# The token-step operations and running sums of a second sequence, placed on other engines and in another step of a one-core Mamba-2 and gated-MLP kernel

## The chip, the cores and the metric

The kernel runs on one core of one Trainium2 chip. A time is the device time of one execution in microseconds (us); the lower the better. TensorE (PE) multiplies matrices, VectorE (DVE), ScalarE (ACT) and GpSimd (POOL) do the element-wise work, and SyncE (SP) issues most transfers. Each engine works through its own instruction stream in order; the streams meet at semaphores alone.

## What is computed

For two sequences of 512 tokens of width 512, `x` is normalised, and then `x + s * silu(ffn)` is formed. `ffn` is a gated MLP with four-bit weights. `s` is a Mamba-2 layer with 128 heads of 64 channels in 8 groups. Cut to what matters here:

```python
proj = hidden_states @ in_proj_w.T
gate, xBC, dt = jnp.split(proj, [INTER, INTER + CONV_DIM], axis=-1)
xBC = silu(causal_conv(xBC, conv_w, 4) + conv_b)
x, Bm, Cm = jnp.split(xBC, ...)
dt = jnp.clip(jax.nn.softplus(dt + dt_bias), 0.001, 100.0)
dA = dt * A                      # A = -(1 .. 128), one per head
cs = jnp.cumsum(dA, axis=-1)     # within chunks of 128 tokens
scores = (C @ B.T) * where(tril, exp(cs_l - cs_s), 0)
Y = scores @ (x * dt) + C @ states * exp(cs) + x * D
out = rmsnorm_per_group(Y * silu(gate)) * norm_w @ out_proj_w.T
```

The change concerns `dt`, `dA` and `cs` of the second sequence.

## The kernel before

A **body** is one of 16 pairs of sequence and head group (the two sequences alternate), and a body has eight **steps** `k` of 128 channels (two heads) each; `n = 8 * body + k` numbers the steps. Each engine has a function `step(body, k)`, and `over_bodies` (line 96) calls it for n = 0, 1, 2, ... on every engine. All matrices that meet weights are split into a high and a low part, so that one product is three matmuls (`split_mm`, line 140).

In a step TensorE does, in order: `y_off` (L590, L573 in the trace, the state's share of the output of the step before), `conv` (the projection for three steps ahead, L143 to L145), `y_diag` (`diag`, L609, and `state_mm`, L573), `gate_mm` (the gate two steps ahead), `out_mm` (L677 to L679), `extra` (at k = 3 and 4 the B and C projections of the next body, at 6 and 7 more small ones) and `turn_x` (L738). At n = 2 and 3 the order differs a little (lines 765 to 774): at n = 2 there is no `out_mm`, and at n = 3 `second_values` (L808, transposes L805) stands ahead of `y_diag`, and two `out_mm` follow `gate_mm`.

VectorE does in a step: `xdt`, `xw` and `ec` (L1306, L1309, L1315), then at n = 1 `token_steps(dve, 1)`, at n = 2 `smallest` once (L1267), at n = 3 `stage_hp(1)` (L1443) and `smallest` twice; then `inner` (L1360, writes `yt`), the state recurrence (L1379, L1384), `taps_x_conv` (L1246, three multiply-adds), at n = 1 `cumulate(1)`, and last, in the crowded steps n = 1, 2 and 3, `scores` (L1280).

`token_steps(eng, b)` (line 352) is three operations on 128x512 numbers of sequence `b`: the sum that completes the softplus (L356), the clip (L359) and the product with A (L362). It waits for `pa` (ScalarE's logarithm, `soft_ln(1)`, L1076, at n = 0) and `pd` (VectorE's `relu_dt(1)`, ahead of the steps). `cumulate(b)` (line 1430) is four scans of 128x128 (L1433), one for each chunk; they raise `pd`.

Who waits for the scans:

- ScalarE, in `first_steps` at k = 2: after `raw_x_conv` (L1000) and `round_x` (L901) comes `send_sums(1)` (line 1078), which waits for all scans and issues the transfer of `cs` to `cs_d`; then `decays(1)` (L1083, four L1085, and the transfer to `e_d`), then `work_a` (L964, eight exponentials for the scores), `round_out`, `rest`. At k = 3 come `stage_hp(1)` (L1096), `raw_x_conv`, `round_x`, `work_a` and so on; `gate_raw` (L987) moves a gate out of PSUM and raises `gev_done`.
- GpSimd, at n = 1, between the low part of the convolution's weights (L1611) and that of the gate's (L1627): `pool.wait_ge(pd, SEQS * N_PD)`, with no work behind it. At n = 2 `weigh(1)` (L1549: L1551, L1553) waits for `pa` (that is, for `decays(1)`) and `pd`.
- TensorE, at n = 3: `second_values` waits for `wg_done`, that is for `weigh(1)`.

GpSimd does in a step: `gated` (L1594, L1598), L1611, the low parts of the B and C, gate and output weights (L1620, L1627, L1631), the sum of squares (L1604) and `low_y` (L1578, which raises `lo_done`). VectorE's `inner(k)` writes `yt[k % 2]` and so waits for the `low_y` that read it (`lo_done`, line 1358), besides TensorE's `diag` (`yd_done`).

Of the kernel before, what the change touches and what calls it, by code (L numbers as in the profile page):

```python
# [26 lines left out]
SEQS, SEQ, DIM = 2, 512, 512  # L27
# [52 lines left out]
def at(body, k, d):  # L80

    k += d
    return body.plus(k // TILES), k % TILES


def wait(eng, sem, count):

    if isinstance(count, int) and count <= 0:
        return
    eng.wait_ge(sem, count)  # L90
# [18 lines left out]
def paired(n):  # L109

    return TILES // 2 <= n < TILES * (BODIES - 1) + TILES // 2
# [47 lines left out]
def build(nc, x, w_conv, w_gate, w_out, w_dt, conv_p, norm_p, head_p, consts, w1q, w1s, w3q, w3s,  # L159
# [9 lines left out]
    with ExitStack() as ctx:  # L169
        def sem(name):  # L170
            return ctx.enter_context(nc.semaphore(name))
# [112 lines left out]
        pd = sem("pd")  # L284
# [67 lines left out]
        def token_steps(eng, b):  # L352

            eng.wait_ge(pa, (N_SOFT + N_EXPS) * b + N_SOFT)
            eng.wait_ge(pd, N_PD * b + 1)
            eng.tensor_tensor(qt[Q_DT][:, half[b], :], qt[Q_DT][:, half[b], :], ecs[:, half[b], :],  # L356
                              ALU.add).then_inc(dt_done, 1)
            eng.wait_ge(dt_done, 3 * b + 1)
            eng.tensor_scalar(qt[Q_DT][:, half[b], :], qt[Q_DT][:, half[b], :], DT_MIN, DT_MAX, ALU.max,  # L359
                              ALU.min).then_inc(dt_done, 1)  # L360
            eng.wait_ge(dt_done, 3 * b + 2)
            eng.tensor_scalar(qt[Q_CD][:, half[b], :], qt[Q_DT][:, half[b], :], heads[:, 2:3], None,  # L362
                              ALU.mult).then_inc(dt_done, 1)
# [4 lines left out]
        N_PD = 1 + NC  # L368
# [21 lines left out]
        def sq_tile(kp):  # L390

            return sq_sum[:, :] if kp == 0 else gate[:, kp % 4, :]
# [845 lines left out]
        def _(dve):  # L1238
# [21 lines left out]
            def smallest(body, k):  # L1260
                bd, kr = at(body, k, 2)
                if bd.exists():
                    m = TILES * bd.n + kr
                    if kr == 0:
                        wait_hp(dve, bd)
                    dve.wait_ge(row_in[m % LM_BUFS], 16 * (m // LM_BUFS + 1))
                    dve.scalar_tensor_tensor(lm[m % LM_BUFS][:, :, :],  # L1267
                                             hp[bd.seq][:, Q_CS, kr, :].unsqueeze(2).broadcast_to((P, 2 * NC, CHUNK)),
                                             -1.0, lm[m % LM_BUFS][:, :, :], ALU.mult, ALU.min).then_inc(min_done, 1)
# [13 lines left out]
            def step(body, k):  # L1283
                n = TILES * body.n + k
# [53 lines left out]
                                                 ALU.mult, ALU.add).then_inc(acc_done, 1)  # L1338

                if n == 1:  # L1340
                    token_steps(dve, 1)
                elif n == 2:
                    smallest(body, 1)
                elif n == 3:
                    stage_hp(1)
                    smallest(body, 2)
                    smallest(body, 3)
                else:
                    smallest(body, k)
# [13 lines left out]
                def taps_x_conv():  # L1363
                    bd, kx = at(body, k, 3)
                    if bd.exists():
                        taps(bd, X_POS[kx], z[:, kx % 2, :], ps_a, tap0_x, taps_x, TILES * bd.n + kx)
# [23 lines left out]

                if not (paired(n) and k % 2):
                    taps_x_conv()
                if n == 1:
                    cumulate(1)
                if crowded:
                    scores(body, k)
# [33 lines left out]
            def cumulate(b):  # L1430
                dve.wait_ge(dt_done, 3 * (b + 1))
                for c in range(NC * b, NC * b + NC):
                    dve.tensor_tensor_scan(qt[Q_CS][:, c, :], ones[:, :], qt[Q_CD][:, c, :], 0.0, ALU.mult,  # L1433
                                           ALU.add).then_inc(pd, 1)

            def stage_hp(b):
                if b:
                    dve.wait_ge(hp_out, 16 * b)
                for q in (Q_DT, Q_DEC):
                    dve.wait_ge(qt_tr, NQ * b + q + 1)  # L1440
                    if b == 0:
                        dve.wait_ge(hp0_ev, q + 1)
                    dve.tensor_copy(stage[:, q, :, :, :].rearrange("p g k (j c) -> p c (g k) j", c=NC),  # L1443
                                    qt_bank[q][:, :].rearrange("p (c u j) -> p c u j", c=NC, j=2)).then_inc(qt_ev, 1)
# [90 lines left out]
        def _(pool):  # L1535
# [45 lines left out]
            def step(body, k):  # L1581
                n = TILES * body.n + k
                pv, kp = at(body, k, -1)
                before = body.plus(-1)
                if k == 1 and before.exists():
                    pool.wait_ge(rs_done, before.n + 1)
                    wait(pool, acc_done, NC * before.n)
                    pool.tensor_tensor(rstd[:, :], rstd_sum[:, :], neg_half[:, 0:NC], ALU.pow).then_inc(rv_done, 1)
                chain_late = paired(n) and k % 2

                def gated():
                    pool.wait_ge(t0_done, n)
                    pool.wait_ge(y1_done, n)
                    pool.tensor_tensor(yt[:, kp % 2, P:SEQ], yt[:, kp % 2, P:SEQ], ec[kp % 2][:, :], ALU.add  # L1594
                                       ).then_inc(add_done, 1)
                    pool.wait_ge(gs_done, n)
                    pool.wait_ge(add_done, n)
                    pool.tensor_tensor(yt[:, kp % 2, :], yt[:, kp % 2, :], gate[:, kp % 4, :], ALU.mult  # L1598
                                       ).then_inc(yg_done, 1)

                def sum_sq():
                    pool.wait_ge(sq_done, n)
                    wait(pool, sqa_done, (TILES - 1) * pv.n + kp - 1)
                    pool.tensor_tensor(sq_sum[:, :], sq_sum[:, :], sq_tile(kp), ALU.add).then_inc(sqa_done, 1)  # L1604

                if pv.exists() and not chain_late:
                    gated()
                bd, kx = at(body, k, 4)
                if bd.exists():
                    pool.wait_ge(whi_x, TILES * bd.n + kx + 1)  # L1610
                    pool.tensor_tensor(conv_lo[kx % 2][:, :, :],  # L1611
                                       raw_x[:, kx % 2, :].rearrange("p (k j) -> p k j", k=KT),
                                       conv_hi[kx % 2][:, :, :].bitcast(F32), ALU.subtract).then_inc(wlo_x, 1)
                if paired(n) and k == 0:
                    sum_sq()
                if n == 2:
                    weigh(1)
                for bd, i in bc_piece(body, k):
                    pool.wait_ge(whi_b, 2 * bd.n + i + 1)
                    pool.tensor_tensor(conv_lo[2][:, :, :], bc_raw(bd).rearrange("p (k j) -> p k j", k=KT),  # L1620
                                       conv_hi[2][:, :, :].bitcast(F32), ALU.subtract).then_inc(wlo_b, 1)
                if n == 1:

                    pool.wait_ge(pd, SEQS * N_PD)
                for group, pos in gate_piece(body, k):
                    pool.wait_ge(whi_g, 8 * group + pos + 1)
                    pool.tensor_tensor(gate_lo[pos // 4][:, pos % 4, :], raw_g[:, :],  # L1627
                                       gate_hi[pos // 4][:, pos % 4, :].bitcast(F32), ALU.subtract).then_inc(wlo_g, 1)
                for group, pos in out_piece(body, k):
                    pool.wait_ge(whi_o, TILES * group + pos + 1)  # L1630
                    pool.tensor_tensor(wout_lo[pos // 4][:, pos % 4, :], raw_o[:, :],  # L1631
                                       wout_hi[pos // 4][:, pos % 4, :].bitcast(F32), ALU.subtract).then_inc(wlo_o, 1)
                if chain_late:
                    gated()
                low_first = (body.is_number(BODIES - 1) and k >= 5) or body.is_number(BODIES) or chain_late
                if low_first and pv.exists():
                    low_y(body, k)
                if pv.exists() and kp > 0 and body.exists() and not (paired(n) and k == 0):
                    sum_sq()
                if pv.exists() and not low_first:  # L1640
                    low_y(body, k)
                if k == 6 and body.is_number(0):
                    pool.wait_ge(hp_out, 16 * SEQS)
                    pool.wait_ge(qt_tr, NQ * SEQS)
                    pool.memset(acc[:, :, :], 0.0).then_inc(zero_done, 1)
# [156 lines left out]
```

## Time and profile before

| | us |
|---|---|
| median of 3 runs | 1759.21 (1757.86 to 1759.34) |
| the profiled execution's own time | 1758.21 |
| its span in the trace | 1756.4 |
| TensorE busy | 1742.4 (99%) |
| VectorE busy | 1402.7 (80%) |
| ScalarE busy | 1221.6 (70%) |
| GpSimd busy | 1232.1 (70%) |

All rows come from the one profiled execution, whose time is 1.8 us above its span. The start times in a timeline count from the span's start. Instructions of one engine overlap by some 0.06 to 0.1 us in the records, so distances between starts say more than sums of durations.

### The profile page before, as it was taken

The page shows a single profiled execution, that of the slowest core. Times are in us where ns is not written, and L with a number is a line of the kernel's source. Part 1 is how long each engine was busy: PE and PEld are TensorE (multiplying, and loading weights), DVE is VectorE, ACT ScalarE, POOL GpSimd, SP SyncE. Part 2 cuts the span into 40 slices and gives each one's busy share as a digit, 9 for nine tenths or more (in the row PEclk, how much of TensorE's full clock was granted, in tenths as well). Part 3 has the DMA queues.
Part 4 walks back from the last instruction along what each step waited for, and adds up shares of the span by engine and source line. Part 5 has one row for each costly group of instructions (what it writes and reads, how often), then busy time and mean ns, then how long its engine had stood idle before and what let it go on. Part 6 is the DMA issues. An engine that isn't in the chain of part 4 may idle for free.

```text
span 1756.4 us, 30305 instructions
## 1 busy us (share of the span) xinstructions
PE 1742.4 (99%) x10301; PEld 1459.3 (83%) x10301; DVE 1402.7 (80%) x2211; ACT 1221.6 (70%) x2456; POOL 1232.1 (70%) x877
## 2 busy tenths in 40 slices
PE   8999999999999999999999999999999999999999
PEld 6788888888888888888888888888888888888877
DVE  7978788878878788778788788878887887868941
ACT  6986677777776777777867778767877787643320
POOL 5677777777876787677776777677777787576630
PEclk9999999999999999999999999999999999999999
DMA  5442333333333343333333333333323343236522
GB/s 196 165 131 99 116 116 112 98 123 109 134 105 94 104 135 109 108 101 117 118 102 118 116 111 108 103 109 127 123 91 103 109 135 107 76 98 175 146 78 96
DMA packets 122595, 202.84 MB, mean 115 GB/s; under 512 B 23056, under 2 KB 60560, under 8 KB 122192
## 3 DMA queue, kind: packets, MB, share of 16 engines
q1 hardware_dynamic: 120720, 197.32, 34.8%
q10 hardware_dynamic: 1728, 3.65, 0.5%
q8 instruction: 82, 1.34, 0.3%
q14 instruction: 65, 0.53, 0.1%
HBM read 193.57 MB, written 7.34 MB: 114 GB/s over the span
## 4 chain that ended last, share of the span: by engine, by line
PE 94%; DVE 3%; issue 1%; POOL 1%; DMA 0%; ACT 0%; SPq 0%; DVEq 0%; ACTq 0%; POOLq 0%
PE bank L143 17%; PE bank L145 16%; PE bank L144 16%; PE bank L573 10%; PE bank L609 7%; PE bank L677 7%; PE bank L679 7%; PE bank L678 6%; PE bank L888 3%; PE bank L738 3%; DVE z L1246 1%; PE bank L700 0%; DVE lm L1267 0%; PE bank L720 0%; DVE acc L1337 0%
## 5 line engine op out<-in xcount | busy, mean ns | idle before, releaser
L964 ACT ACTIVATE lm<-lm,hp 128x128 f32<-128x128 f32 x1024 | 313.1, 389 | 0.8
L1246 DVE SCALAR_TENSOR_TENSOR z<-bank,cw_all,z 128x511 f32<-128x511 f32 (+2 forms) x384 | 286.9, 747 | 13.3 <-ACT z L1000 4.2
L1611 POOL TENSOR_TENSOR conv_lo<-raw_x,conv_hi 128x512 fp32r<-128x512 f32 x124 | 203.7, 1643 | 129.4 <-ACT conv_hi L901 129.3
L143 PE MATMUL bank<-xn_hi,conv_hi 128*128 128x512 f32 x640 | 261.4, 408 | 1.9 <-DVE z L1246 1.4
L1306 DVE TENSOR_TENSOR xdt<-bank,hp 128x512 f32<-128x512 f32 x128 | 88.2, 689 | 212.4 <-PE bank L738 212.4
L145 PE MATMUL bank<-xn_hi,conv_lo 128*128 128x512 f32 x640 | 250.6, 392 | 0.0
L144 PE MATMUL bank<-xn_lo,conv_hi 128*128 128x512 f32 x640 | 249.5, 390 | 0.0
L1594 POOL TENSOR_TENSOR yt<-yt,ec 128x384 f32<-128x384 f32 x128 | 146.8, 1147 | 139.3 <-DVE ec L1315 107.9
L1280 DVE SCALAR_TENSOR_TENSOR lm<-lm,gm 128x1024 f32<-128x1024 f32 x128 | 225.3, 1760 | 7.8 <-ACT lm L964 7.2
L1578 POOL TENSOR_TENSOR y_lo<-yt,y_hi 128x512 fp32r<-128x512 f32 x128 | 180.1, 1407 | 52.4 <-ACT y_hi L1035 52.4
L143 PE MATMUL bank<-xn_hi,gate_hi 128*128 128x512 f32 x512 | 212.9, 416 | 0.0
L677 PE MATMUL bank<-wout_hi,y_hi 128*128 128x512 f32 x512 | 206.1, 403 | 0.0
L1598 POOL TENSOR_TENSOR yt<-yt,gate 128x512 f32<-128x512 f32 x128 | 192.1, 1500 | 18.9 <-POOL yt L1594 0.9
L1604 POOL TENSOR_TENSOR sq_sum<-sq_sum,gate 128x512 f32<-128x512 f32 x111 | 172.7, 1556 | 40.3 <-ACT gate L1041 40.2
L679 PE MATMUL bank<-wout_hi,y_lo 128*128 128x512 f32 x512 | 200.8, 392 | 0.0
L144 PE MATMUL bank<-xn_lo,gate_hi 128*128 128x512 f32 x512 | 200.3, 391 | 0.0
L145 PE MATMUL bank<-xn_hi,gate_lo 128*128 128x512 f32 x512 | 200.2, 391 | 0.0
L678 PE MATMUL bank<-wout_lo,y_hi 128*128 128x512 f32 x512 | 199.5, 390 | 0.0
L987 ACT ACTIVATE gate<-bank 128x512 f32<-128x512 f32 x128 | 75.0, 586 | 173.4 <-PE bank L145 173.4
L1267 DVE SCALAR_TENSOR_TENSOR lm<-hp,lm 128x1024 f32<-128x1024 f32 x128 | 185.9, 1453 | 0.0
L1000 ACT ACTIVATE z<-bank,cw_all 128x512 f32<-128x512 f32 x128 | 98.6, 770 | 101.8 <-PE bank L145 100.9
L145 PEld LDWEIGHTS bank<-xn_hi,conv_lo 128*128 128x128 f32 x640 | 120.1, 188 | 26.6
(152 smaller groups left out, 4051.5 us busy)
## 6 DMA issues: line engine op xcount, KB each, us to landing
lm<-cs_d SPq DMA_DIRECT2D x128, 512.0 KB, 4.5
raw_x<-w_conv_dram SPq DMA_DIRECT2D x128, 256.0 KB, 3.5
ec<-e_d SPq DMA_DIRECT2D x256, 96.0 KB, 2.7
raw_o<-w_out_dram SPq DMA_DIRECT2D x64, 256.0 KB, 3.0
raw_g<-w_gate_dram SPq DMA_DIRECT2D x61, 256.0 KB, 3.2
raw_g<-w_conv_dram SPq DMA_DIRECT2D x16, 256.0 KB, 3.2
raw_o<-w_conv_dram SPq DMA_DIRECT2D x14, 256.0 KB, 3.4
q_raw<-w1q_dram SPq DMA_DIRECT2D x10, 256.0 KB, 3.9
```

Of the source, the lines that this page charges most:

```text
L143: pe.matmul(dst, a_hi, b_hi, start=(i == 0), stop=False)
L144: pe.matmul(dst, a_hi, b_lo, start=False, stop=False)
L145: mm = pe.matmul(dst, a_lo, b_hi, start=False, stop=(i == len(terms) - 1))
L677: pe.matmul(ps_o[c][:, :], y_hi[:, ko % 2, o], w[0], start=first, stop=False)
L678: pe.matmul(ps_o[c][:, :], y_hi[:, ko % 2, o], w[1], start=False, stop=False)
L679: mm = pe.matmul(ps_o[c][:, :], y_lo[:, ko % 2, o], w[0], start=False, stop=last)
L964: e = act.activation(lm[m % LM_BUFS][:, u, :], lm[m % LM_BUFS][:, u, :], ACT.Exp, bias=hp[bd.seq][:, Q_CS, k1, u:u + 1])
L1246: dve.scalar_tensor_tensor(dst[:, d:SEQ], src[:, 0:SEQ - d], cw_all[:, bd.group, pos, 3 - d:4 - d], dst[:, d:SEQ], ALU.mult, ALU.add).then ...
L1267: dve.scalar_tensor_tensor(lm[m % LM_BUFS][:, :, :], hp[bd.seq][:, Q_CS, kr, :].unsqueeze(2).broadcast_to((P, 2 * NC, CHUNK)), -1.0, lm[m ...
L1280: dve.scalar_tensor_tensor(lm_c, lm_c, 1.0, gm[:, :, :].rearrange("p c l -> p (c l)").unsqueeze(1) .broadcast_to((P, 2, SEQ)), ALU.mult, A ...
L1598: pool.tensor_tensor(yt[:, kp % 2, :], yt[:, kp % 2, :], gate[:, kp % 4, :], ALU.mult).then_inc(yg_done, 1)
L1611: pool.tensor_tensor(conv_lo[kx % 2][:, :, :], raw_x[:, kx % 2, :].rearrange("p (k j) -> p k j", k=KT), conv_hi[kx % 2][:, :, :].bitcast(F ...
```

## The change

At n = 1 the three operations of `token_steps` of the second sequence leave VectorE's stream and stand in GpSimd's, where its wait for the scans stood; that wait is gone. VectorE's four scans of that sequence stand in n = 2 and not in n = 1: behind the taps, ahead of `scores`. ScalarE's, TensorE's and SyncE's streams are the same.

```diff
@@ VectorE, step
                 if n == 1:
-                    token_steps(dve, 1)
+                    pass
                 elif n == 2:
                     smallest(body, 1)
@@ VectorE, step, behind the state recurrence
                 if not (paired(n) and k % 2):
                     taps_x_conv()
-                if n == 1:
+                if n == 2:
                     cumulate(1)
                 if crowded:
                     scores(body, k)
@@ GpSimd, step
                 if n == 1:
-
-                    pool.wait_ge(pd, SEQS * N_PD)
+                    token_steps(pool, 1)
                 for group, pos in gate_piece(body, k):
```

## Rows read from the trace of the kernel before

**Rows 1.** The page: TensorE's busy time, its share and its instructions.
```profile
PE 1742.4 (99%) x10301; PEld 1459.3 (83%) x10301; DVE 1402.7 (80%) x2211; ACT 1221.6 (70%) x2456; POOL 1232.1 (70%) x877
```
**Rows 2.** Waits of TensorE, 40 to 300 us: total, times, longest.
```profile
PE bank L143 <- DVE z L1246: 1.4, 2, 0.9
PE bank L609 <- DVE ec L1315: 0.8, 1, 0.8
PE bank L738 <- DVE state L1384: 0.5, 1, 0.5
```
**Rows 3.** Windows: stretch, busy PE, PEld, DVE, ACT, POOL; granted clock, DMA, GB/s.
```profile
82.00:94.00 12.00, 12.00 (x59) 9.82 (x59) 7.96 (x13) 11.69 (x28) 10.64 (x7) 1.00 0.55 194
```
**Rows 4.** Timeline of VectorE, sequence 0's scans, then n = 1 to 2: start, us, line.
```profile
21.99 1.37 DVE L1433 TENSOR_TENSOR_SCAN qt<-ones,qt 128x128 f32<-128x128 f32 x4
...
56.77 0.68 DVE L356 TENSOR_TENSOR qt<-qt,ecs 128x512 f32<-128x512 f32 x1
...
59.96 0.73 DVE L1360 SCALAR_TENSOR_TENSOR yt<-xt,dc_all,bank 128x512 f32<-128x512 f32 x1
60.62 0.28 DVE L1379 COPY state<-bank 128x128 f32<-128x128 f32 x1
...
64.06 1.36 DVE L1433 TENSOR_TENSOR_SCAN qt<-ones,qt 128x128 f32<-128x128 f32 x4
65.34 1.20 DVE L1280 SCALAR_TENSOR_TENSOR lm<-lm,gm 128x1024 f32<-128x1024 f32 x1
...
67.98 2.01 DVE L1267 SCALAR_TENSOR_TENSOR lm<-hp,lm 128x1024 f32<-128x1024 f32 x1
71.25 0.75 DVE L1360 SCALAR_TENSOR_TENSOR yt<-xt,dc_all,bank 128x512 f32<-128x512 f32 x1 [1.25 <-issue]
...
75.36 1.73 DVE L1280 SCALAR_TENSOR_TENSOR lm<-lm,gm 128x1024 f32<-128x1024 f32 x1
```
**Rows 5.** Timeline of TensorE: products of n = 1, diagonal of n = 2, projection of n = 3.
```profile
58.38 1.09 PE L609 MATMUL bank<-lm,xdt 128*64 128x128 f32 x16
59.40 0.94 PE L573 MATMUL bank<-xw,b_tok 128*128 128x128 f32 x6
...
68.12 1.09 PE L609 MATMUL bank<-lm,xdt 128*64 128x128 f32 x16 [0.83 <-DVE ec L1315]
...
90.26 0.50 PE L143 MATMUL bank<-xn_hi,conv_hi 128*128 128x512 f32 x1
```
**Rows 6.** Timeline of GpSimd: one cast ahead of the steps, then n = 1.
```profile
40.21 0.61 POOL L1568 CAST gate_hi<-raw_g 128x512 fp32r<-128x512 f32 x1 [1.07 <-DMA raw_g<-w_gate_dram]
...
59.86 1.32 POOL L1611 TENSOR_TENSOR conv_lo<-raw_x,conv_hi 128x512 fp32r<-128x512 f32 x1
65.50 2.18 POOL L1627 TENSOR_TENSOR gate_lo<-raw_g,gate_hi 128x512 fp32r<-128x512 f32 x1 [4.32 <-DVE qt L1433]
...
68.88 2.27 POOL L1578 TENSOR_TENSOR y_lo<-yt,y_hi 128x512 fp32r<-128x512 f32 x1
```
**Rows 7.** Timeline of ScalarE: sequence 0's wait for its scans; then n = 1 to 3.
```profile
23.78 2.06 ACT L1057 ACTIVATE xn_hi<-bank 128x512 fp32r<-128x512 f32 x4 [1.24 <-DVE qt L1433]
...
63.45 0.61 ACT L928 ACTIVATE gate_hi<-raw_g 128x512 fp32r<-128x512 f32 x1
...
68.53 0.62 ACT L1083 ACTIVATE ecs<-qt 128x512 f32<-128x512 f32 x1
...
70.22 2.44 ACT L964 ACTIVATE lm<-lm,hp 128x128 f32<-128x128 f32 x8
...
79.99 2.09 ACT L1096 ACTIVATE stage<-bank 128x512 f32<-128x512 f32 x2 [1.03 <-PE bank L805]
...
89.63 0.58 ACT L987 ACTIVATE gate<-bank 128x512 f32<-128x512 f32 x1
```
**Rows 8.** Timeline of TensorE ahead of the steps: transposes at the kernel's start, and later.
```profile
4.05 4.60 PE L816 MATMUL bank<-ident 128*128 128x128 f32 x24 [4.05 <-DMA ident<-consts_dram]
...
21.05 1.91 PE L787 MATMUL bank<-ident,x_in 128*128 128x128 f32 x16
```

## The prediction

> **What bounds the kernel now.** I read the page first: TensorE is busy for 99% of the span [rows 1], so time is won or lost only where TensorE stands still, or comes to stand still. The list of TensorE's waits between 40 and 300 us comes next [rows 2]: four stalls, 2.7 us in all, and all of them before 76 us, in steps n = 1 to 3, where the change lies. Each is put down to VectorE. From 82 us on TensorE is busy without a break and at a granted clock of 1.00, its upper level of 2.4 GHz, but ScalarE is busy there too, for 11.69 of 12 us [rows 3]. The reader is to see that two engines are full at once behind the change: TensorE, and ScalarE, which feeds it.
>
> So I looked for the point where they meet. In step 3 TensorE starts the B projection of the next body at 90.26 us [rows 5]; it needs PSUM that ScalarE's `gate_raw` empties, and that instruction ends at 89.63 + 0.58 = 90.21 [rows 7]. ScalarE comes just in time: whatever makes it later than this makes TensorE later by the same amount. How much can ScalarE lose before that point? Between 68.53 and there its only idle time is 1.03 us at 79.99 [rows 7], where it waits for TensorE's transposes of the second sequence; I count 1.1 with the overlap of records.
>
> **The change, part by part.**
>
> *Step 1, VectorE.* The three operations begin at 56.77 and `inner` behind them at 59.96, so 3.2 us go [rows 4]. Little of it is kept at once: `inner` waits for the diagonal products, which end at 58.38 + 1.09 = 59.5, and the state copy waits for the state products, 59.40 + 0.94 = 60.35 [rows 5], where it stood at 60.62 [rows 4]. The scans go too. The scores then start at 60.38 + (64.06 - 60.62) = 63.8 and not at 65.34: 1.5 us earlier. The stall of 0.8 us ahead of the diagonal [rows 2] should go: `ec`, now 0.05 ahead of the diagonal at 68.12 [rows 5], moves with the scores to 66.5, before the projection ends at 67.2.
>
> *Step 1, GpSimd.* After L1611 ends at 61.2 it now works where it waited 4.32 us [rows 6]. The trace has no large `tensor_scalar` on GpSimd. The first operation, with two inputs, is like L1611, 1.3. For the two with one input I take the cast of the same size, 0.61 each, with 1.3 as the upper end; 0.61 is nearest, since it too reads one tensor and writes one. That gives 61.2 + 1.3 + 1.2 = 63.7, and the next piece, L1627, can't start before ScalarE's rounding ends at 64.06 [rows 7] anyway. At the upper end it starts at 65.1, still before the 65.50 of now.
>
> The trace shows something dearer. L1627 lasts 2.18 where it meets VectorE's scores (65.34 to 66.54), L1578 lasts 2.27 where it meets `smallest` of 2.01 [rows 4, 6]: such pairs run one after the other. So I put them in turn: scores to 65.0, L1627 to 66.3, the output weights (1.3) to 67.5, `smallest` to 68.7, L1578 to 69.9. The two bounds: no such meeting, 67.9; operations of 1.3 us, with scores between them, 71.0. The Trainium skill states this in "GPSIMD Engine Reference", Key points: the SBUF interfaces are shared with VectorE, in contention with its instructions with two SBUF inputs. By that rule the trace agrees, 2.18 and 2.27 against 1.32. The same page's Engine selection speaks against moving such work: GpSimd takes about twice as long for two inputs and is near line rate for one; by it, as an estimate, the three would take what I took at the lower end.
>
> *Step 2, VectorE.* Its `inner` starts now at 71.25, just behind L1578's end at 71.15 [rows 4, 6]. In the new kernel that end is 69.9, not below 68.4 (the diagonal, at 68.12 behind 0.83 of idleness now, starts at 67.3 and takes 1.09 [rows 5]), not above 71.1 by the sum above. From `inner` to the end of the taps is 75.36 - 71.25 = 4.1 [rows 4]: 74.0. There the scans stand now, 1.36 [rows 4]: they end at **75.4 (73.9 to 76.6)**.
>
> *Step 2, ScalarE.* This is the cost. Its stream did not change: behind L901 it waits for the scans before it sends the sums. They ended at 65.4 and it went by at 68.53 without a stop [rows 4, 7]. Now it stands from 68.6 until 75.4. Everything behind the wait stands with it: the decays, eight exponentials, output weights, silus, `y_hi`, `gate_raw`. From the end of the scans to its next work are 0.42 us for sequence 0 (scans to 23.36, issue of the transfer, next activation at 23.78 [rows 4, 7]); from the decays to the exponentials 70.22 - 68.53 = 1.69. So the exponentials start at 75.4 + 0.4 + 1.7 = 77.5, for 70.22 now: **ScalarE is 7.3 us late (5.8 to 8.5)**.
>
> *Step 3.* Who waits: GpSimd's `weigh`, for the decays; TensorE's 16 transposes for `weigh`; VectorE's scores for the exponentials (until 80.0), and behind them xdt, xw and ec; so the diagonal of n = 3 starts near 83 instead of 80.3, and the next gate projection near 85.8 instead of 82.0 for `gate_raw` of n = 2. None of it is the last. ScalarE's idle 1.1 at 79.99 is gone, since the transposes are done by 82: it is 6.2 late (4.7 to 7.4) from there on, and `gate_raw` of n = 3 ends at 96.4. TensorE's two `out_mm` end near 94, so it waits for ScalarE, and starts the B projection 6.2 us late. The two transfers, `cs_d` and `e_d`, are issued 7 us later; their first readers are the rows of body 1, steps away. SyncE's queue waits for GpSimd's and VectorE's counts and shifts with them by no more.
>
> *Behind.* TensorE had no idle time from 82 us on to win the delay back [rows 2, 3], and the 2.7 us of stalls that VectorE no longer causes lie ahead of the new, longer waits and are swallowed by them. The sum: +6.2 us, 1758.21 + 6.2 = 1764.4 against the profiled execution. That one lies 1.0 below the median of the runs; I add half of that: **1764.9 us**.
>
> **The rivals.**
>
> *VectorE is what counts, and the change helps.* All of TensorE's stalls here are put down to VectorE [rows 2], and 4.5 us leave its step 1. If ScalarE's stop costs nothing, the three later stalls vanish (0.8, 0.5 and the longer one of 0.9): -2.3 us, 1756.4 by my base, the same within measurement. It decides at the scans' end: by 69.7 (68.6 plus the 1.1 of slack) ScalarE loses nothing. Against it: `inner` alone can't start before 68.4, and 5.5 us of VectorE's work stand behind it. Chance 0.12, most of it for a reading of mine of who waits that is wrong.
>
> *GpSimd's one-input operations are slow.* At 3 us each they end at 68.5; L1627, the output weights and L1578 follow with one meeting, 73.2; `inner` then, scans to 78.7, ScalarE 9.5 us late after its slack: 1768.2. For: only tiny ones are in the trace. Against: the cast, 0.61 [rows 6]. Chance 0.12.
>
> *TensorE's clock falls in the new gaps.* It would stand for 2 us several times between 77 and 96. The first 24 transposes, after TensorE had stood still from the start, took 4.60 us; at 1.91/16 each they take 2.87 [rows 8]. A start from rest costs 1.7, and only the last gap's counts, the earlier ones being behind ScalarE: +7.9, 1766.6. Against: between the gaps it works for 8 us. "TensorE: Matmul & The Clock Gate" (the Trainium skill, What's actually happening) has the slow clock come back after idleness; no row here shows it inside the work. Chance 0.05.
>
> *The change doesn't do what it says*, because ScalarE meets the scans earlier than I order them: that is the first rival, as the stream order is plain in the diff.
>
> **How the numbers follow.** My forecast has 0.71. With its bounds it alone spans 1758.7 + 4.7 to 1758.7 + 7.4 = 1763.4 to 1766.1; half a microsecond to a whole one of spread between runs and the slow-GpSimd case widen it upward to 1768.0, downward a part hidden by something I have not seen, to 1762.0. A measurement tells about 0.2% here, 3.5 us: all but the first rival and a thin edge of the forecast are slower by more. Faster by over 0.2% has 0.02, within 0.2% 0.13, slower 0.85.
>
> **What would show it.** In the profile of the changed kernel: scans near 74 to 75.4; ScalarE idle for 6 to 7 us ahead of L1083, released by L1433, as it was 1.24 for sequence 0 [rows 7]; three GpSimd lines at 61.2 to 64; next to no idle ahead of L1627; TensorE waiting before the transposes L805, the diagonal, a gate projection and the B projection, together some 9 us in place of 2.3; from then on every row as before, 6.2 us later. The forecast is wrong if ScalarE's wait is there and TensorE's B projection starts near 90 all the same, or if the scans end before 70.

## The result, and the profile after

The changed kernel takes 1767.2 us (median of 6 runs, 1765.57 to 1767.99) against 1758.85 for the kernel before (6 runs, 1757.86 to 1760.19): a ratio of 1.0046, 95% interval 1.0033 to 1.0059. It is slower by 8 us, and the direction, the place and the mechanism are those of the forecast of 1764.9 (1762.0 to 1768.0), with the size short by 2.3 us.

The page of the changed kernel, span and busy times. TensorE has the same work (1743.7 us busy for 1742.4) in a span 9.7 us longer:

```profile
span 1766.1 us, 30304 instructions
PE 1743.7 (99%) x10301; PEld 1460.2 (83%) x10301; DVE 1400.7 (79%) x2208; ACT 1221.7 (69%) x2456; POOL 1235.1 (70%) x880
```

TensorE's waits in the changed kernel (total, times, longest), of the whole span; they answer to [rows 2]. The wait for ScalarE's `gate` and most of those for `state` and `qt` are new:

```profile
PE bank L143 <- ACT gate L987: 3.2, 2, 2.0
PE bank L738 <- DVE state L1384: 2.8, 2, 1.7
PE bank L805 <- POOL qt L1553: 2.7, 2, 2.3
PE bank L143 <- DVE z L1246: 1.4, 2, 0.9
PE bank L609 <- DVE ec L1315: 1.3, 1, 1.3
```

The timeline of ScalarE (start, us, line, operation, idle time before and what ended it), for [rows 7]. It stands for 8.8 us ahead of the decays, until the scans are done; the idle 1.03 ahead of L1096 is gone; `gate_raw` of n = 3 begins 8.3 us later than before:

```profile
78.03 0.63 ACT L1083 ACTIVATE ecs<-qt 128x512 f32<-128x512 f32 x1 [8.82 <-DVE qt L1433]
79.74 2.43 ACT L964 ACTIVATE lm<-lm,hp 128x128 f32<-128x128 f32 x8
88.37 2.02 ACT L1096 ACTIVATE stage<-bank 128x512 f32<-128x512 f32 x2
97.94 0.57 ACT L987 ACTIVATE gate<-bank 128x512 f32<-128x512 f32 x1
```

The timeline of TensorE, the first projection matmul of n = 1 and the B projection of n = 3, for [rows 5]:

```profile
56.28 0.47 PE L143 MATMUL bank<-xn_hi,conv_hi 128*128 128x512 f32 x1 [0.46 <-DVE z L1246]
...
98.57 0.50 PE L143 MATMUL bank<-xn_hi,conv_hi 128*128 128x512 f32 x1 [2.04 <-ACT gate L987]
```

All of the first body is 0.8 us late in this execution, ahead of the change (56.28 for 55.48 us). The cause stands at the start of VectorE's timeline: the statistics of one of the first tiles of `x` wait for its transfer. First the kernel before, then the changed one:

```profile
6.16 0.69 DVE L1404 BATCH_NORM_STATS2 bn<-x_in 128x6 f32<-128x512 f32 x1 [0.16 <-DMA x_in<-x_dram]
```

```profile
6.92 0.69 DVE L1404 BATCH_NORM_STATS2 bn<-x_in 128x6 f32<-128x512 f32 x1 [0.84 <-DMA x_in<-x_dram]
```

In seven of the experiments this row stands between 6.11 and 7.31 us, and in all nine executions the first matmul of n = 1 follows 49.3 to 49.5 us behind it. The 24 opening transposes [rows 8] vary too (5.29 us here for 4.60), but they don't set it: they last 4.49 us in e9_scans_early_held and 5.38 in e3_scans_early, and both start n = 1 at 56.0. There is one profile for each kernel, so whether this lateness has to do with the kernel is not shown; it lies ahead of the change.

So I read distances inside the body. From the first to the second of these two rows I call **D**. D was 90.26 - 55.48 = 34.8 us; it is now 42.3: **7.5 us more, in a stretch in which the matmuls are the same.**

The timeline of VectorE, for [rows 4]: `smallest`, `inner`, the scans and the scores of n = 2. Inner starts at 72.16, that is 71.4 in the clock of before; the scans last 1.36 us and end at 77.6; the scores stand for 4.57 us behind ScalarE's exponentials:

```profile
67.32 2.34 DVE L1267 SCALAR_TENSOR_TENSOR lm<-hp,lm 128x1024 f32<-128x1024 f32 x1
72.16 0.75 DVE L1360 SCALAR_TENSOR_TENSOR yt<-xt,dc_all,bank 128x512 f32<-128x512 f32 x1 [2.50 <-issue]
...
76.26 1.36 DVE L1433 TENSOR_TENSOR_SCAN qt<-ones,qt 128x128 f32<-128x128 f32 x4
82.20 1.23 DVE L1280 SCALAR_TENSOR_TENSOR lm<-lm,gm 128x1024 f32<-128x1024 f32 x1 [4.57 <-ACT lm L964]
```

The timeline of GpSimd, for [rows 6]. The two `tensor_scalar` last 1.93 and 1.98 us, where VectorE took 1.13 and 1.39 for them in n = 1; they end at 67.3, `low_y` (L1578) at 72.06, and `inner` starts 0.1 behind it:

```profile
63.33 1.93 POOL L359 TENSOR_SCALAR qt<-qt 128x512 f32<-128x512 f32 x1
65.35 1.98 POOL L362 TENSOR_SCALAR qt<-qt,heads 128x512 f32<-128x512 f32 x1
67.30 1.28 POOL L1626 TENSOR_TENSOR gate_lo<-raw_g,gate_hi 128x512 fp32r<-128x512 f32 x1
68.54 2.27 POOL L1630 TENSOR_TENSOR wout_lo<-raw_o,wout_hi 128x512 fp32r<-128x512 f32 x1
70.78 1.28 POOL L1578 TENSOR_TENSOR y_lo<-yt,y_hi 128x512 fp32r<-128x512 f32 x1
```

### The profile page after: what moved, and what is told of

Its sections match the earlier page's. It is cut to its first block, busy times and chain, and to the rows that moved or that the text cites. A ratio compares the mean times of both kernels' runs of the same rounds, so it can differ in the third digit from the quotient of the medians.

```text
span 1766.1 us, 30304 instructions
## 1 busy us (share of the span) xinstructions
PE 1743.7 (99%) x10301; PEld 1460.2 (83%) x10301; DVE 1400.7 (79%) x2208; ACT 1221.7 (69%) x2456; POOL 1235.1 (70%) x880
## 4 chain that ended last, share of the span: by engine, by line
PE 89%; DVE 3%; POOL 2%; ACT 2%; issue 2%; DMA 1%; SPq 0%; ACTq 0%; POOLq 0%; DVEq 0%
PE bank L143 16%; PE bank L145 16%; PE bank L144 16%; PE bank L573 10%; PE bank L609 6%; PE bank L677 6%; PE bank L679 6%; PE bank L678 6%; PE bank L888 3%; PE bank L738 3%; ACT lm L964 1%; DVE z L1246 1%; POOL conv_lo L1611 0%; DMA raw_g<-w_gate_dram 0%; PE bank L700 0%
## 5 line engine op out<-in xcount | busy, mean ns | idle before, releaser
L1594 POOL TENSOR_TENSOR yt<-yt,ec 128x384 f32<-128x384 f32 x128 | 145.5, 1136 | 138.9 <-DVE ec L1315 107.5
L1578 POOL TENSOR_TENSOR y_lo<-yt,y_hi 128x512 fp32r<-128x512 f32 x128 | 180.1, 1407 | 52.6 <-ACT y_hi L1035 52.6
L1598 POOL TENSOR_TENSOR yt<-yt,gate 128x512 f32<-128x512 f32 x128 | 191.6, 1497 | 18.4
L143 PEld LDWEIGHTS bank<-xn_hi,conv_hi 128*128 128x128 f32 x640 | 120.6, 188 | 26.2 <-ACT gate L987 2.5
```

The source lines that it names most:

```text
L143: pe.matmul(dst, a_hi, b_hi, start=(i == 0), stop=False)
```

## The experiments

The theories. **A**: the cost is ScalarE's stop for the late scans. **B**: it is GpSimd's slower operations and what they hold back. **C**: TensorE waits for the second sequence's weights, whatever ScalarE does. After the first four runs came theory **D** (D without the word "theory" is always the distance): GpSimd and a VectorE operation with two inputs in SBUF take turns, so that where the scans stand decides what they last.

### The three operations alone on GpSimd (e1_tokens_only)

```diff
-                if n == 2:
+                if n == 1:
                     cumulate(1)
```

> The changed kernel with the scans back in n = 1: the three operations on GpSimd alone. Measure D = from the first matmul of the projection of n = 1 (L143) to that of the B projection of n = 3: 34.8 us before, 42.3 in the changed kernel. Theory A (the cost is ScalarE's stop for the late scans): the scans end some 1.5 us before ScalarE asks for them, no stop, D 34 to 35.5, time within 1.5 us of before. Rival B (the cost is GpSimd's slower operations and what they delay: output weights, low_y): most of the 7.5 us stay, D 40 or more.

Measured: 1763.97 us (8 runs) against 1759.24 of before in the same series (26 runs), ratio 1.0028 (1.0017 to 1.0039), +4.7 us; the distance D = 96.78 - 56.15 = 40.6, 5.8 more than before. A's numbers are missed and B's is met, though not by B's mechanism. The timelines of GpSimd, VectorE, ScalarE and TensorE:

```profile
63.16 1.93 POOL L359 TENSOR_SCALAR qt<-qt 128x512 f32<-128x512 f32 x1
65.18 1.58 POOL L362 TENSOR_SCALAR qt<-qt,heads 128x512 f32<-128x512 f32 x1
...
66.80 4.49 DVE L1433 TENSOR_TENSOR_SCAN qt<-ones,qt 128x128 f32<-128x128 f32 x4 [2.22 <-POOL qt L362]
...
71.69 0.63 ACT L1083 ACTIVATE ecs<-qt 128x512 f32<-128x512 f32 x1 [2.65 <-DVE qt L1433]
...
73.99 1.98 PE L609 MATMUL bank<-lm,xdt 128*64 128x128 f32 x16 [6.28 <-DVE ec L1315]
```

The operations end at 66.7, so VectorE sits idle for 2.2 us; and then the four scans last 4.49 us, not 1.36. Behind them are the scores, the multiplications of n = 2 and `ec`, and TensorE stands for 6.3 us. ScalarE's stop is only 2.65 us, with 1.61 more behind it for `smallest`, and TensorE doesn't wait for ScalarE ahead of the B projection. So this kernel pays in another coin: not what GpSimd does next (its `low_y` begins at 69.3, earlier than in the changed kernel), but VectorE, waiting for GpSimd and then scanning beside it.

### The scans alone in n = 2 (e2_scans_only)

```diff
                 if n == 1:
-                    pass
+                    token_steps(dve, 1)
@@ GpSimd
-                if n == 1:
-                    token_steps(pool, 1)
```

> The changed kernel with the three operations back on VectorE in n = 1 and nothing in their place on GpSimd: the late scans alone. Theory A: VectorE's inner of n = 2 starts about 1.5 us earlier than in the changed kernel, ScalarE still stops for some 6 to 7.5 us, D 40 to 41, +5.5 to +6.5 us over before. Rival B: D 34 to 36, +0 to +1.

Measured: 1764.68 us (7 runs), ratio 1.0035 (1.0024 to 1.0047), +5.4 us; D = 97.06 - 56.13 = 40.9, 6.1 more than before. A holds (its time of +5.5 to +6.5 is missed by 0.1). The timelines of VectorE (`inner` of n = 2) and ScalarE:

```profile
70.65 0.75 DVE L1360 SCALAR_TENSOR_TENSOR yt<-xt,dc_all,bank 128x512 f32<-128x512 f32 x1 [1.25 <-issue]
76.53 0.63 ACT L1083 ACTIVATE ecs<-qt 128x512 f32<-128x512 f32 x1 [7.25 <-DVE qt L1433]
```

`Inner` starts at 70.65 (70.0 in the clock of before, 14.5 behind the first matmul; 15.9 in the changed kernel), ScalarE's stop is 7.25 us. The late scans alone make 6.1 of the 7.5 us. The rest, 1.4, is what `inner` loses by GpSimd's two slow operations.

### The scans ahead of `smallest` in n = 2 (e3_scans_early)

```diff
                 elif n == 2:
+                    cumulate(1)
                     smallest(body, 1)
@@
-                if n == 2:
-                    cumulate(1)
                 if crowded:
```

> The changed kernel with the four scans at another place in n = 2: ahead of smallest, not behind the taps. GpSimd's three operations as in the changed kernel. Theory A: the scans end near 68.7 in that trace's clock, ScalarE's stop shrinks from 8.8 us to under 1, D 34.5 to 35.5, time within 1.5 us of before. Rival B: D 40 or more, since GpSimd does what it does in the changed kernel.

Measured: 1763.31 us (10 runs), ratio 1.0023 (1.0013 to 1.0033), +4.1 us; D = 94.53 - 56.03 = 38.5. Half of the loss came back, not all. The timelines of VectorE (the scans) and TensorE (behind the gate projection of n = 2):

```profile
67.11 5.31 DVE L1432 TENSOR_TENSOR_SCAN qt<-ones,qt 128x128 f32<-128x128 f32 x4
...
76.64 1.09 PE L738 MATMUL bank<-ident,xt 128*128 128x128 f32 x4 [4.37 <-DVE state L1385]
```

The scans begin at 67.1, as meant, and last 5.31 us, 1.17 to 1.50 each. They end at 72.4: ScalarE still stops for 3.9 us, and VectorE is late with all behind them, for which TensorE waits 4.4 us. Neither A nor B had room for that; it started theory D.

### ScalarE does other work first (e5_decays_behind_exps)

```diff
-                if k == 2:
-                    send_sums(1)
-                    decays(1)
                 ...
                 round_out(body, k)
+                if k == 2:
+                    send_sums(1)
+                    decays(1)
                 rest(body, k)
```

> The changed kernel with ScalarE's sending of the sums and its decays of the second sequence placed behind the exponentials and output weights of n = 2, not ahead of them. The scans end as late as in the changed kernel. Theory A: 3.7 us of ScalarE's work move into its stop, which shrinks from 8.8 to about 5.1; D falls by 3.7 to 38.6, the time to +4 to +5 over before. Rival C (TensorE waits for the weights of the second sequence, that is for the decays through GpSimd and the 16 transposes, whatever ScalarE does between): D stays at 42.

Measured: 1762.79 us (10 runs), ratio 1.0021 (1.0012 to 1.0031), +3.6 us; D = 95.08 - 56.36 = 38.7. D is what A says (38.6), the time a little under its +4 to +5, and C falls: the scans end as late as ever (77.7 for 77.6), the weights pass through the decays, GpSimd and TensorE as late as ever (the transposes L805 start at 81.90 for 81.78), and half of the loss is gone. ScalarE's timeline ahead of the decays:

```profile
73.60 0.72 ACT L943 ACTIVATE raw_o<-raw_o,nw_all 128x512 f32<-128x512 f32 x1 [1.36 <-DMA raw_o<-w_out_dram]
...
78.13 0.63 ACT L1083 ACTIVATE ecs<-qt 128x512 f32<-128x512 f32 x1 [3.15 <-DVE qt L1433]
```

The stop is 3.15, less than the 5.1 expected, but 1.36 us of it moved ahead, where ScalarE now waits for a load, and 0.5 ahead of the exponentials.

### GpSimd held while VectorE scans (e9_scans_early_held)

e3_scans_early and one line:

```diff
                 if n == 1:
                     token_steps(pool, 1)
+                    pool.wait_ge(pd, SEQS * N_PD)
```

> As e3_scans_early, with GpSimd's wait for the scans put back behind its three operations in n = 1, so that GpSimd does nothing while VectorE scans. Theory D (the two engines take turns: a scan with two inputs in SBUF lets one GpSimd operation through each, 1.3 us a scan): the four scans take 1.4 us and not 5.3; GpSimd's next pieces start later (68.5 in place of 67.0), yet D (from the first matmul of the projection of n = 1 to that of the B projection of n = 3) falls from 38.5 to about 36.4, time +1 to +2.5 over before. Rival E (the scans were slow for what they read, freshly written by GpSimd): they still take 4 us or more and D is 39 to 40.

Measured: 1761.02 us (11 runs) against 1758.94 (23 runs), ratio 1.0014 (1.0005 to 1.0023), +2.1 us; D = 92.26 - 55.99 = 36.3. A wait was added, and D fell from 38.5 to 36.3 and the time from +4.1 to +2.1. The intervals of the two ratios overlap, so that it gains rests on D more than on the times. The timelines of VectorE and TensorE:

```profile
67.06 1.37 DVE L1432 TENSOR_TENSOR_SCAN qt<-ones,qt 128x128 f32<-128x128 f32 x4
...
70.73 0.50 PE L143 MATMUL bank<-xn_hi,gate_hi 128*128 128x512 f32 x1 [1.27 <-POOL gate_lo L1626]
75.38 0.63 PE L738 MATMUL bank<-ident,xt 128*128 128x128 f32 x4 [1.64 <-DVE state L1385]
```

The same scans on the same data, written by GpSimd as before, last 1.37 us: rival E falls, theory D holds. The price of the hold is in the two other rows: TensorE waits 1.3 us for GpSimd's low part of the gate weights and 1.6 for the state.

### The kernel before without GpSimd's wait (e4_no_wait)

```diff
-                if n == 1:
-
-                    pool.wait_ge(pd, SEQS * N_PD)
```

> The kernel before with one line taken away: GpSimd's wait for the scans in n = 1. It doesn't idle the 4.3 us. Theory D: the scans, 1.36 us now, meet three GpSimd operations and take 3.5 to 5 us; VectorE is 2 to 3.5 us late in n = 2 and the diagonal of n = 2 with it; D 36 to 38, time +1 to +3. Rival F (the wait was only a cost): scans 1.4 us, low_y earlier, D 33.5 to 34.5, time -1.

Measured: 1761.72 us (11 runs), ratio 1.0018 (1.0009 to 1.0027), +2.8 us; D = 94.46 - 56.02 = 38.4, against 36 to 38 expected. The timelines of VectorE, GpSimd and TensorE:

```profile
64.59 4.50 DVE L1433 TENSOR_TENSOR_SCAN qt<-ones,qt 128x128 f32<-128x128 f32 x4
...
64.69 1.41 POOL L1624 TENSOR_TENSOR gate_lo<-raw_g,gate_hi 128x512 fp32r<-128x512 f32 x1 [2.97 <-ACT gate_hi L928]
66.06 1.42 POOL L1628 TENSOR_TENSOR wout_lo<-raw_o,wout_hi 128x512 fp32r<-128x512 f32 x1
67.43 1.38 POOL L1578 TENSOR_TENSOR y_lo<-yt,y_hi 128x512 fp32r<-128x512 f32 x1
...
71.80 1.98 PE L609 MATMUL bank<-lm,xdt 128*64 128x128 f32 x16 [3.96 <-DVE ec L1315]
```

Three GpSimd operations run beside the scans and are hardly slower (1.41, 1.42, 1.38 for 1.29), while the scans take 4.50 for 1.36: the first, ahead of them, 0.41, the other three 1.42 to 1.46, one scan for each operation. The diagonal runs at the lower clock (1.98 us for 1.09), which no theory had. The wait of 4.32 us in [rows 6], which looks like pure loss, was worth 2.8 us; without it GpSimd still stands for 2.97, until ScalarE's rounding.

### The scans in VectorE's idle time (e7_scans_behind_smallest)

```diff
                 elif n == 2:
                     smallest(body, 1)
+                    cumulate(1)
@@
-                if n == 2:
-                    cumulate(1)
                 if crowded:
```

> The changed kernel with the scans behind smallest in n = 2, where VectorE sat idle for 2.5 us waiting for low_y. Theory D: GpSimd works there too (output weights, low_y, the gated output), so the scans take 4 to 5 us instead of 1.4; they end near 74.5, ScalarE's stop is some 6 us and inner is 2 to 3 us late; D 39 to 41. Rival: they fill the idle time at 1.4 us, end near 71.2, D 37 or less.

Measured: 1764.34 us (6 runs), ratio 1.0030 (1.0018 to 1.0042), +5.4 us; D = 96.29 - 56.69 = 39.6. VectorE's timeline:

```profile
69.98 5.35 DVE L1432 TENSOR_TENSOR_SCAN qt<-ones,qt 128x128 f32<-128x128 f32 x4
```

As theory D says (D 39 to 41; the scans last 0.35 more than its 4 to 5): they fill the 2.5 us of idleness and 2.8 more, and ScalarE stops for 6.1. The idleness was not free: GpSimd worked in it.

### The first sequence's operations on GpSimd (e6_tokens0_pool)

```diff
-            token_steps(dve, 0)
@@ GpSimd, ahead of its wait for sequence 0's scans
+            token_steps(pool, 0)
```

> The kernel before with the three operations of the FIRST sequence on GpSimd, which stands idle there for 5.0 us, while VectorE has nothing with two SBUF inputs to do behind norm. For their durations alone: if GpSimd's tensor_scalar is slow by itself, they last 1.9 and 1.6 us here as well, against 0.43 and 0.49 on VectorE; if the 1.9 of the changed kernel came from meeting VectorE, some 0.6 to 1.3. The first B and C pieces come 3 to 4 us later, part of it hidden by TensorE's weightless matmuls.

One run, 1762.67 us, against 1758.94 of before. GpSimd's timeline, with VectorE idle through the second and the third:

```profile
22.70 1.93 POOL L359 TENSOR_SCALAR qt<-qt 128x512 f32<-128x512 f32 x1
24.73 1.58 POOL L362 TENSOR_SCALAR qt<-qt,heads 128x512 f32<-128x512 f32 x1
```

1.93 and 1.58 us with nothing on VectorE beside them, the same as in e1_tokens_only, where the first met VectorE's taps. VectorE has 0.43 and 0.49 for the two at the same place. `tensor_scalar` on GpSimd is slow by itself; of the changed kernel's 3.9 us only 0.4 comes from meeting VectorE.

### `low_y` ahead of the output weights (e10_low_y_first)

```diff
+                if n == 1:
+                    low_y(body, k)
                 for group, pos in out_piece(body, k):
                 ...
-                if pv.exists() and not low_first:
+                if pv.exists() and not low_first and n != 1:
```

> The kernel before with GpSimd's low_y of n = 1 ahead of its output weights instead of behind them; the wait for the scans stays. In the kernel before VectorE's inner of n = 2 starts at 71.25, 1.25 us after it could, behind low_y. Theory A (TensorE and ScalarE bound this stretch together): inner starts 1.0 to 1.3 us earlier, TensorE's stalls of 0.5 and 0.9 us ahead of the state and the projection shrink, and D falls by at most ScalarE's idle 1.0: 33.7 to 34.8 us, time 0 to -1. Rival: the output weights come 1.3 us later and with them the next load, ScalarE waits for it, D 35 to 36.

Measured: 1758.79 us (11 runs) against 1758.85 (15 runs), ratio 1.0000 (0.9991 to 1.0009); D = 90.44 - 55.45 = 35.0. The timelines of VectorE, ScalarE and TensorE:

```profile
69.88 0.73 DVE L1360 SCALAR_TENSOR_TENSOR yt<-xt,dc_all,bank 128x512 f32<-128x512 f32 x1
...
73.90 0.72 ACT L943 ACTIVATE raw_o<-raw_o,nw_all 128x512 f32<-128x512 f32 x1 [1.31 <-DMA raw_o<-w_out_dram]
...
90.44 0.50 PE L143 MATMUL bank<-xn_hi,conv_hi 128*128 128x512 f32 x1 [0.78 <-ACT gate L987]
```

`Inner` starts 1.4 us earlier and nothing is won: ScalarE waits 1.31 us for the load that now comes later, and TensorE 0.78 for ScalarE. The rival of the expectation is what happened. It agrees with what the argument rests on: time given to VectorE here is worth nothing unless ScalarE gets it too. Time taken from VectorE is another thing: in e4_no_wait ScalarE stands for only 0.34 and 1.61 us, TensorE never waits for it, and D is 3.7 us longer all the same. No kernel of this study is faster than the one before.

## Why the prediction was right, and its size short

**What bounds the kernel.** Right. ScalarE meets TensorE at `gate_raw` of n = 3: TensorE's B projection waits for ScalarE for 2.04 us in the changed kernel (row 98.57), and e5_decays_behind_exps, which touches ScalarE's order alone, moves D by 3.6 us.

**VectorE, step 1.** Right that little is kept: it waits 2.70 us for the diagonal of n = 1, and the stall of 0.8 us ahead of the diagonal of n = 2 is gone.

**GpSimd, step 1. Here the prediction failed in size.** "For the two with one input I take the cast of the same size, 0.61 each, with 1.3 as the upper end." They last 1.93 and 1.58 alone, about three times the value taken and above the upper end. The cast was the nearest row in size, and not near in kind. L1627 starts at 67.3, that is 66.5 in the clock of before, for 65.0 forecast; behind it come one meeting with VectorE that GpSimd pays for (L1630, 2.27 us), as forecast, and `low_y`, which ended at 72.06, 71.3 in the clock of before, for 69.9 forecast; the upper bound of 71.0 was crossed by 0.3. The rival of slow one-input operations had the right sign, at 3 us each too much.

**VectorE and ScalarE, step 2.** Right in every distance: from `inner` to the scans' start 76.26 - 72.16 = 4.1; scans 1.36; from their end to the next activation 0.4; 1.7 to the exponentials. With `inner` 1.5 us later than forecast, the scans end at 76.8 in the clock of before (75.4 forecast), the exponentials start at 78.9 (77.5), 8.7 us late (7.3). e2_scans_only, which has no such operations on GpSimd, gives the forecast itself: `inner` at 70.0 (69.9), D 6.1 longer (6.2).

**Step 3.** Right. ScalarE is 8.7 us late at the exponentials and 7.6 at L1096 (88.37 - 0.8 for 79.99): the 1.1 us of slack. TensorE's four waits are where they were listed, ahead of the transposes, the diagonal, a gate projection and the B projection: 2.3, 1.3, 1.1 and 2.0 us. One reading was wrong without harm to the sum: the 2.7 us of stalls that VectorE causes did not go. The 0.8 ahead of the diagonal went, but that ahead of `turn_x` grew from 0.53 to 1.74, as `inner` starts later, and those of the projections stayed (0.46 and 0.93). They lie ahead of the waits for ScalarE, as the prediction says, and are swallowed.

**The sum.** +6.2 was forecast. With the two operations at their measured length the same sum gives 6.2 + 1.4 = 7.6, and D grew by 7.5. The two profiled executions differ by 9.7 us in span, and that is accounted for: 0.8 in the opening, 7.5 in D, and 1.3 in two stalls at VectorE between 800 and 1100 us (1.1 and 0.6, where before has one of 0.4). Those last come and go: the first is 0.4 to 0.9 in four of the experiments and missing in five. This execution, 1767.99, is the slowest of the six; the medians differ by 8.35 (the ratio's interval makes 5.8 to 10.4 us), and the 0.8 us above D is within what these two vary by.

**The range.** The forecast's own span, from its bounds, ended at 1766.1. The median of 1767.2 lies above that, and inside the range only by the margin added for the spread of runs and for slow GpSimd operations. So that the forecast holds as a number owes something to luck; that the place and the order of the waits hold does not.

**The rivals.** "VectorE is what counts" falls by e10_low_y_first and the result. TensorE's clock stayed at 1.00 through the gaps of the changed kernel's profiled execution, so that rival did not come to pass there, though it did in some experiments (below). Two of the six executions have a mean granted clock of 0.998 and not 1.000, which may be such a fall; their times, 1767.49 and 1767.17, don't stand out. What I had not seen at all: that the scans could take anything but 1.36 us. In the changed kernel they don't, since GpSimd waits for the decays where they now stand; 9 us earlier, in e3_scans_early, they took 5.31, and my expectation there missed.

## What to carry to other kernels

An engine whose own stream a change leaves alone can pay for it all: look for the first instruction on every engine that waits for the moved one, and count that engine's idle time up to where it meets the bound engine. A wait in which one of GpSimd and VectorE stands idle may be what keeps the other fast: before taking it away, list the VectorE operations with two inputs in SBUF, and its `tensor_scalar`, that would then run beside GpSimd. And take a price from a row of the same operation, or leave its upper end open.

## What the runs showed of the hardware

**One small VectorE operation for each GpSimd operation.** A 128x128 scan lasts 0.40 us alone and 1.2 to 1.5 where GpSimd has work: four scans 1.36 us against 4.49, 4.50, 5.31 and 5.35. That each waits for a GpSimd operation to end fits the counts: e1_tokens_only and e4_no_wait have three operations beside the four scans, three scans are slow in each, and the fourth lasts 0.39 and 0.41. The same turns cost a 128x1024 operation at most 1.1 us (2.34 for 1.21), so the price goes by the number of operations, not by their size. The Trainium skill's "GPSIMD Engine Reference" (Key points) says that the SBUF interfaces are shared, in contention with VectorE's instructions with two SBUF inputs or in a 2-port mode; by that the runs agree, and the four-fold length is what they add.

Not only operations with two inputs are slower beside GpSimd. VectorE's two `tensor_scalar` of `token_steps`, with one input in SBUF, last 0.43 and 0.49 us for the first sequence, while GpSimd stands idle. In n = 1 of the kernel before, beside GpSimd's L1594 and L1598, they last this (timeline of VectorE):

```profile
57.49 1.13 DVE L359 TENSOR_SCALAR qt<-qt 128x512 f32<-128x512 f32 x1
58.65 1.39 DVE L362 TENSOR_SCALAR qt<-qt,heads 128x512 f32<-128x512 f32 x1
```

No experiment takes GpSimd's work away there, so the cause is read from the rows alone. The taps, with an input in PSUM, last 2.31 us for three both beside an idle GpSimd (61.83 us, before) and beside a busy one (74.04 us, changed kernel).

**GpSimd's `tensor_scalar`** on 128x512 numbers: 1.93 us with clip (two constants) and 1.58 with a per-partition factor, against 0.61 for its copy and 1.29 for its two-input `tensor_tensor`. The same page of the Trainium skill (Engine selection) calls one-input work roughly line rate; the copy agrees with that, these two don't, and the measurement decides.

**TensorE's clock.** Windows (stretch, busy PE, PEld, DVE, ACT, POOL, granted clock, DMA, GB/s) of e1_tokens_only, around the end of its stall of 6.3 us, where the clock falls to 0.50, the lower level of 1.2 GHz:

```profile
72.00:74.00 2.00, 0.01 (x2) 0.01 (x2) 2.00 (x5) 1.50 (x5) 0.00 (x0) 0.67 0.99 353
74.00:76.00 2.00, 2.00 (x17) 1.67 (x17) 1.07 (x1) 0.90 (x4) 1.91 (x1) 0.50 0.48 182
```

The same of the changed kernel, behind its stalls of 1.7 and 0.9 us; the clock stays at 1.00:

```profile
76.00:78.00 2.00, 1.51 (x7) 1.29 (x8) 1.62 (x5) 0.00 (x0) 0.00 (x0) 1.00 0.09 26
78.00:80.00 2.00, 1.47 (x7) 0.89 (x5) 0.00 (x0) 1.97 (x6) 0.09 (x1) 1.00 0.56 220
```

And of e5_decays_behind_exps, behind stalls of 1.8 and 0.9 us, where it falls:

```profile
76.00:78.00 2.00, 1.40 (x4) 1.15 (x5) 2.00 (x6) 0.00 (x0) 0.00 (x0) 0.67 0.18 50
78.00:80.00 2.00, 2.00 (x6) 1.58 (x5) 2.00 (x4) 1.85 (x6) 0.00 (x0) 0.50 0.51 202
```

In e1_tokens_only the next products run at the lower level. From the diagonal (73.99) to the transposes behind the gate projection are 7.1 us; in the changed kernel the same work takes 4.7 (67.80 to 72.5, its transposes following 1.74 later). The timelines of TensorE, first of e1_tokens_only, then of the changed kernel:

```profile
81.10 0.60 PE L738 MATMUL bank<-ident,xt 128*128 128x128 f32 x4
```

```profile
67.80 1.09 PE L609 MATMUL bank<-lm,xdt 128*64 128x128 f32 x16
74.27 0.63 PE L738 MATMUL bank<-ident,xt 128*128 128x128 f32 x4 [1.74 <-DVE state L1384]
```

So its stall of 6.3 us costs 2.4 more than its length. In e3, e7 and e4, behind stalls of 4.4, 4.4 and 4.0, the windows show 0.50 too. Why two executions with the same short stalls differ is open; no run here tells it.
